# Gathers that read their row numbers from the table of slots, each after a wait on an event of VectorE

## The chip, the cores and the metric

The kernel runs on one core of a Trainium2 chip. The metric is the device time of one execution in microseconds (us), taken as the median of several runs. The core has five engines that run side by side: TensorE (PE in the profile, with PEld for its weight loads), VectorE (DVE), ScalarE (ACT), GpSimd (POOL) and SyncE (SP), the last of which only starts transfers here. They wait for each other by counters (semaphores): `engine.wait_ge(counter, value)`, and `.then_inc(counter, n)` on the instruction that raises it.

## The reference, cut to what matters

```
# x (50000, 128), src (25000,) node of each edge, edge_attr (25000, 128)
h   = relu(layernorm(x))                      # no weights
agg = segment_sum(edge_attr, src, 50000)      # (50000, 128)
g   = silu(concat([h, agg]) @ W1 + b1)        # W1 (256, 256)
g   = g @ W2 + b2                             # W2 (256, 128)
g   = layernorm(g) * ln_gamma + ln_beta
out = x + (g + h)
```

## The kernel before, in words

The nodes are worked through in 49 blocks (`NB`) of 1024 (`BLOCK`), a block as 8 tiles (`TILES`) of 128 rows, in two halves of 4 tiles (`HALF`, `c` = 0 and 1).

**The first stage**, up to about 123 us, sorts the edges: every tile of nodes gets 128 slots, and the table `slot_edge` [128, 392] holds the number of the edge that sits in each slot (one column for each tile), `slot_node` its node. VectorE writes the tables in two pieces (`slot_tables`): the columns of blocks 0 to 2, and all others, during block 0. Each piece raises `slots_ready` by one.

**The main stage** runs over the blocks. For one tile GpSimd fetches 128 rows of `edge_attr` by one indirect DMA (`gather`, L430) into `G`; VectorE makes a matrix of ones and zeros from the node numbers (`one_hots`, `HOT`, L861), and TensorE multiplies the two (`sum_edges`, L602), which gives the sums by node. Beside it ScalarE normalises x (`normalise`, L493) and TensorE turns the result (`turn_h`, L595). Both land in `za` in PSUM. ScalarE copies `za` rounded to `hi` (`split_high`, L500 and L502), VectorE writes the remainder to `lo` (`split_low`, L870). TensorE forms the first layer (`layer1`, L613, L614, L618) and the second (`layer2`, L626 once and L630 for each half), ScalarE the silu (L508) and the sums of squares (L515). VectorE scales (`scale`, L886), adds (`result`, L896), and has the sums with beta and with h (`x_plus_beta`, L853; `residual`, L878). A chain of small dependent operations for the reciprocal roots (`powers`, L729 to L752, one `small` count for each of 13 links) runs on VectorE too, with statistics of the next block (L697), one half of `HOT`, `x_plus_beta` and one `residual` put in between.

VectorE's order in `step(b)` is: `split_low(b, 1)`, `one_hots(b+1, 1)`, `scale(b-2)` for both halves, `result(b-2)` for both halves, `residual(b-1, 1)`, `split_low(b+1, 0)`, `powers(b+2)`. GpSimd does nothing but the gathers in the main stage. It works on block b+2 in its step b, and `G` has three buffers (`RING`), so `gather` waits on `agg_done` until the block three before has been summed. TensorE works on the halves in order; `turn_h` and `sum_edges` of a half stand ahead of `layer1` of the half before. The order on each engine is that of the program.

Around each gather GpSimd first copies one column of the table to a small tile (`name_row`, L418, `gather_rows`), one tile ahead of its use, and the gather waits for `row_named`, which the copy raises. Beside the case shown here there is one for more than 128 edges in a tile (`flag != 0`), which this input doesn't take; it gathers from `spill` by the same function.

Of the kernel before, what the change touches and what calls it, by code (L numbers as in the profile page):

```python
# [10 lines left out]
U32 = mybir.dt.uint32  # L11
# [4 lines left out]
P = 128  # L16
TILES = 8
HALF = TILES // 2
BLOCK = P * TILES
RING = 3  # L20
X_RING = 6
# [12 lines left out]
NEWTON = 3  # L34
# [55 lines left out]
def at_least(engine, semaphore, value):  # L90

    if value > 0:
        engine.wait_ge(semaphore, value)


def gnn_layer(nc, x, src, edge_attr, W1, b1, W2, b2, gamma, beta, out):
# [4 lines left out]
    NB = -(-nodes // BLOCK)  # L101
# [3 lines left out]
    FULL = edges // EC  # L105
    REST = edges - FULL * EC
    FIRST_BLOCKS = 3
    assert all((place + LAG_DVE_RANK) % BATCH == BATCH - 1 for place in DVE_RANKS)
    assert EC % UNROLL == 0 and UNROLL % STREAMS == 0 and NT <= 512

# [3 lines left out]
    with ExitStack() as ctx:  # L114
        def sb(name, shape, dt):
            return ctx.enter_context(nc.sbuf_tensor(name, shape, dt))
# [4 lines left out]
        def sem(name):  # L121
            return ctx.enter_context(nc.semaphore(name))
# [47 lines left out]
        slot_edge = sb("slot_edge", [P, NT], U32)  # L170
# [23 lines left out]
        R = [sb(f"R{j}", [P, TILES, D], F32) for j in range(RING)]  # L194
        G = [sb(f"G{j}", [P, TILES, D], F32) for j in range(RING)]
        HOT = [sb(f"HOT{j}", [P, TILES, P], F32) for j in range(RING)]
        gather_rows = [sb(f"gather_rows{j}", [P, TILES], U32) for j in range(X_RING)]

        hi = [sb(f"hi{c}", [P, 2, HALF * P], F32R) for c in range(2)]
        lo = [sb(f"lo{c}", [P, 2, HALF * P], F32R) for c in range(2)]  # L200
# [35 lines left out]
        spill_known, slots_ready = sem("spill_known"), sem("slots_ready")  # L236
        pool_step = sem("pool_step")
        spill_zeroed, spill_added = sem("spill_zeroed"), sem("spill_added")
        row_named = sem("row_named")
        x_loaded = [sem(f"x_loaded{j}") for j in range(X_RING)]  # L240
        stored = [sem(f"stored{j}") for j in range(RING)]
        gathered = [[sem(f"gathered{j}{c}") for c in range(2)] for j in range(RING)]
        bn_done, small, powers_done = sem("bn_done"), sem("small"), sem("powers_done")
        h0_done, turn_done, hot_done, agg_done = sem("h0_done"), sem("turn_done"), sem("hot_done"), sem("agg_done")
        hi_done, lo_done = sem("hi_done"), sem("lo_done")
        pre_done, silu_done, y_done = sem("pre_done"), sem("silu_done"), sem("y_done")
        squares_done = sem("squares_done")
        xb_done, r_done, t_done, out_done = sem("xb_done"), sem("r_done"), sem("t_done"), sem("out_done")
        pool_passed = sem("pool_passed")

        def run_blocks(step):

            for n in range(NB):
                step(Block(n))
# [68 lines left out]
        def _(pool):  # L323
# [85 lines left out]
                    pool.dma_reset(range(spill_added.num, spill_added.num + 1))  # L409
                    pool.sem_clear(spill_added)  # L410

            def name_row(b, t):

                if t == 0:
                    at_least(pool, agg_done, b.half(0, 1, 2 - 2 * X_RING))
                    if b.is_number(FIRST_BLOCKS):
                        pool.wait_ge(slots_ready, 2)
                nc.gpsimd.tensor_copy(gather_rows[b.xj][:, t:t + 1],  # L418
                                      slot_edge[:, bass.ds(b.number(TILES, t), 1)]).then_inc(row_named, 1)

            def gather(b, c, source, limit):

                at_least(pool, agg_done, b.half(0, 1, 2 - 2 * RING))
                for t in range(c * HALF, (c + 1) * HALF):
                    if t + 1 < TILES:
                        name_row(b, t + 1)
                    elif b.plus(1).exists(NB):
                        name_row(b.plus(1), 0)
                    at_least(pool, row_named, b.number(TILES, t + 1))
                    nc.gpsimd.indirect_dma_start(  # L430
                        G[b.j][:, t, :], None, source,
                        bass.IndirectOffsetOnAxis(ap=gather_rows[b.xj][:, t:t + 1], axis=0),
                        bounds_check=limit, oob_is_err=False).then_inc(gathered[b.j][c], 16)

            def gather_all(source, last):

                limit = pool.to_reg(last)
                for n in range(2):
                    for c in range(2):
                        gather(Block(n), c, source, limit)  # L440

                def step(b):
                    if b.plus(2).exists(NB):
                        for c in range(2):
                            gather(b.plus(2), c, source, limit)

                run_blocks(step)

            pool.wait_ge(late_const, 1)
            pool.wait_ge(slots_ready, 1)  # L450
            name_row(Block(0), 0)
            with pool.If(flag == 0):
                gather_all(edge_attr, edges - 1)
            with pool.If(flag != 0):
# [201 lines left out]
        def _(dve):  # L656
# [35 lines left out]
            def statistics(b, t):  # L692
# [4 lines left out]
                done = nc.vector.bn_stats(stats[b.ring(2)][:, t, :], X[b.xj][:, t, :])  # L697
                if t == TILES - 1:
                    done.then_inc(bn_done, 1)

            SMALLS = 4 + 3 * NEWTON

            def powers(b):

# [4 lines left out]
                def link_small(instruction):  # L709
# [8 lines left out]
                    if b.plus(-2).exists(NB) and not b.is_number(0) and not b.is_number(1):  # L718
                        if place in (TILES + 1, TILES + 2):
                            x_plus_beta(b.plus(-2), place - TILES - 1)  # L720
                        if place == TILES + 3:
                            residual(b.plus(-2), 0)
                    dve.wait_ge(small, b.number(SMALLS, count[0]))

# [120 lines left out]
            dve.wait_ge(words_placed, 2)  # L845
            slot_tables(0, FIRST_BLOCKS * TILES)

# [9 lines left out]
            def one_hots(b, c):  # L857
                if b.is_number(FIRST_BLOCKS) and c == 0:
                    dve.wait_ge(slots_ready, 2)
# [46 lines left out]
            def step(b):  # L906
# [3 lines left out]
                if b.is_number(0):  # L910
                    slot_tables(FIRST_BLOCKS * TILES, NT)
                elif not b.is_number(1):
# [43 lines left out]
```

## Time and profile before

| | us |
|---|---|
| median of 3 runs (800.46 to 802.87) | 801.94 |
| the profiled execution, its own time | 803.43 |
| its span, first to last instruction | 801.9 |
| PE busy (share of the span) | 733.6 (91%) |
| DVE busy | 732.1 (91%) |
| ACT busy | 587.0 (73%) |
| POOL busy | 601.1 (75%) |
| mean granted TensorE clock | 0.974 |

Busy is the time in which an engine has at least one instruction under way; neighbours on one engine overlap by some hundredths of a us. A matmul's end is modelled, so a busy PE isn't PE at its peak. The span is cut into stretches below, since the first 123 us (the sorting) are another program than the rest.

### The profile page before, as it was taken

The numbers are of one execution on the slowest core, as the hardware profiler recorded it, in microseconds if no ns is written. First come the engines' busy times: TensorE is split into PE (matmuls) and PEld (weight loads), VectorE is DVE, ScalarE is ACT, GpSimd is POOL, SyncE is SP. The second block draws the span as 40 slices with busy tenths as digits, with TensorE's granted clock in tenths as the row PEclk, the third lists the DMA queues.
The fourth block names the chain that finished last, engine by engine and source line by source line (L and its number), as shares of the span: only waits on it lengthen the run. The fifth ranks groups of instructions, "written<-read, shape, count | busy, mean of one in ns | idle before, by whom it ended". The sixth has DMA issues, their size and how long they took to land.

```text
span 801.9 us, 15882 instructions
## 1 busy us (share of the span) xinstructions
PE 733.6 (91%) x4567; PEld 592.4 (74%) x4616; DVE 732.1 (91%) x2494; ACT 587.0 (73%) x1927; POOL 601.1 (75%) x831
## 2 busy tenths in 40 slices
PE   4999993989999999999999999999999999989990
PEld 1455542878888888888888888888888888878880
DVE  6999995879999999999999999999999999989994
ACT  4999982767777777777777777777777777757860
POOL 4600006889998999889989998999989998989920
PEclk9999995999999999999999999999999999999996
DMA  5000000122323333332323232323233332321211
GB/s 191 2 1 2 1 0 17 48 74 75 124 90 110 98 103 99 102 120 80 126 74 126 74 125 74 127 78 121 91 107 100 102 107 93 126 66 51 71 61 48
DMA packets 28159, 65.86 MB, mean 82 GB/s; under 512 B 8379, under 2 KB 9934, under 8 KB 28070
## 3 DMA queue, kind: packets, MB, share of 16 engines
q1 hardware_dynamic: 15526, 51.90, 18.6%
q0 software_dynamic: 12544, 12.93, 6.5%
q8 instruction: 37, 0.61, 0.3%
q14 instruction: 52, 0.43, 0.2%
HBM read 51.98 MB, written 25.60 MB: 97 GB/s over the span
## 4 chain that ended last, share of the span: by engine, by line
POOL 66%; ACT 10%; issue 8%; PE 8%; DVE 5%; DMA 1%; SPq 0%; POOLq 0%; DVEq 0%
POOL G L430 50%; POOL gather_rows L418 16%; ACT junk_rank L472 10%; PE y L630 2%; PE za L602 1%; PE pre L613 1%; PE pre L614 1%; DVE hot_tile L768 1%; PE pre L618 1%; DVE hot_slot L790 1%; DVE T L886 1%; DMA srci<-in_src_dram 1%; DMA G<-in_edge_attr_dram,gather_rows 1%; PE za L595 0%; DVE is_slot L781 0%
## 5 line engine op out<-in xcount | busy, mean ns | idle before, releaser
L430 POOL DMA_INDIRECT G<-in_edge_attr_dram,gather_rows x392 | 440.6, 1124 | 63.4 <-POOL gather_rows L418 48.2
L418 POOL COPY gather_rows<-slot_edge 128x1 uint32<-128x1 uint32 x392 | 138.5, 354 | 92.0 <-DVE slot_edge L842 89.6
L630 PE MATMUL y<-w2c,S 128*128 128x128 f32 x1568 | 190.9, 275 | 3.3
L630 PEld LDWEIGHTS y<-w2c,S 128*128 128x128 f32 x1568 | 191.5, 192 | 2.5
L493 ACT ACTIVATE H<-X,shift,rstd 128x128 f32<-128x128 f32 x392 | 162.4, 508 | 7.7 <-DVE shift L752 7.6
L613 PE MATMUL pre<-hi,w1h 128*128 128x512 f32 x392 | 164.8, 420 | 0.4 <-issue 0.4
L870 DVE TENSOR_TENSOR lo<-za,hi 128x1024 fp32r<-128x1024 f32 x98 | 119.8, 1222 | 46.5 <-ACT hi L502 42.3
L614 PE MATMUL pre<-hi,w1l 128*128 128x512 f32 x392 | 156.1, 398 | 0.0
L500 ACT CAST hi<-za 128x512 fp32r<-128x512 f32 x98 | 57.4, 586 | 123.5 <-PE za L595 113.6
L602 PE MATMUL za<-HOT,G 128*128 128x128 f32 x784 | 114.4, 290 | 18.4 <-issue 10.1
L508 ACT ACTIVATE S<-pre,b1c 128x512 f32<-128x512 f32 x196 | 125.3, 697 | 5.0 <-remote 2.1
L602 PEld LDWEIGHTS za<-HOT,G 128*128 128x128 f32 x784 | 97.1, 195 | 37.4 <-DMA G<-in_edge_attr_dram,gather_rows 31.5
L618 PE MATMUL pre<-lo,w1h 128*128 128x512 f32 x392 | 124.0, 397 | 0.0
L697 DVE BATCH_NORM_STATS2 stat<-X 128x6 f32<-128x128 f32 x392 | 109.0, 284 | 0.0
L515 ACT ACTIVATE junk_sq<-y 128x128 bf16<-128x128 f32 x392 | 103.7, 286 | 3.5 <-PE y L630 3.5
L886 DVE SCALAR_TENSOR_TENSOR T<-y,rstd,gammas 128x128 f32<-128x128 f32 x392 | 105.6, 341 | 0.0
L502 ACT CAST hi<-za 128x512 fp32r<-128x512 f32 x98 | 57.6, 588 | 42.4 <-PE za L602 25.0
L618 PEld LDWEIGHTS pre<-lo,w1h 128*128 128x128 f32 x392 | 74.4, 190 | 18.1
L613 PEld LDWEIGHTS pre<-hi,w1h 128*128 128x128 f32 x392 | 75.0, 191 | 14.3 <-issue 0.8
L515 ACT ACTIVATION_READ_ACCUMULATOR junk_sq<-y 128x1 f32 x392 | 85.0, 217 | 0.0
L614 PEld LDWEIGHTS pre<-hi,w1l 128*128 128x128 f32 x392 | 75.0, 191 | 13.4
L595 PE MATMUL za<-ident,H 128*128 128x128 f32 x392 | 59.8, 276 | 13.4 <-ACT H L493 9.0
(123 smaller groups left out, 1047.3 us busy)
## 6 DMA issues: line engine op xcount, KB each, us to landing
X<-in_x_dram SPq DMA_DIRECT2D x48, 512.0 KB
out_dram<-R SPq DMA_DIRECT2D x48, 512.0 KB
G<-in_edge_attr_dram,gather_rows POOLq DMA_INDIRECT x392
X<-in_x_dram SPq DMA_DIRECT2D x1, 424.0 KB
out_dram<-R SPq DMA_DIRECT2D x2, 212.0 KB
w1f<-in_L_gnn_W_dram SPq DMA_DIRECT2D x1, 256.0 KB, 3.3
w2f<-in_L_gnn_W_dram SPq DMA_DIRECT2D x1, 128.0 KB, 2.6
srci<-in_src_dram SPq DMA_DIRECT2D x1, 97.2 KB
```

Source lines behind the costliest of these rows:

```text
L418: nc.gpsimd.tensor_copy(gather_rows[b.xj][:, t:t + 1], slot_edge[:, bass.ds(b.number(TILES, t), 1)]).then_inc(row_named, 1)
L430: nc.gpsimd.indirect_dma_start(G[b.j][:, t, :], None, source, bass.IndirectOffsetOnAxis(ap=gather_rows[b.xj][:, t:t + 1], axis=0), bounds_ ...
L493: done = nc.scalar.activation(H0[b.j][:, t, :], X[b.xj][:, t, :], ACT.Relu, bias=shift[b.j][:, t:t + 1], scale=rstd[b.j][:, t:t + 1])
L508: nc.scalar.activation(S[c][:, m, :], pre[m][:], ACT.Silu, bias=b1c[:, m:m + 1]).then_inc(silu_done, 1)
L515: done = nc.scalar.activation(junk_sq[:, p, c * HALF + t, :], y[2 * p + c][:, t * D:(t + 1) * D], ACT.Square, scale=float(D) ** -0.5, accu ...
L602: done = nc.tensor.matmul(za[:, 1, t * P:(t + 1) * P], G[b.j][:, c * HALF + t, :], HOT[b.j][:, c * HALF + t, :], start=True, stop=True)
L613: nc.tensor.matmul(pre[m][:], w1h[:, k, cols], hi[c][:, k, :], start=(k == 0), stop=False)
L614: nc.tensor.matmul(pre[m][:], w1l[:, k, cols], hi[c][:, k, :], start=False, stop=False)
L618: done = nc.tensor.matmul(pre[m][:], w1h[:, k, cols], lo[c][:, k, :], start=False, stop=(k == 1))
L630: done = nc.tensor.matmul(place[:, t * D:(t + 1) * D], S[c][:, m, t * P:(t + 1) * P], w2c[:, m, :], start=False, stop=(t == HALF - 1 and m ...
L870: nc.vector.tensor_tensor(out=lo[c][:], in0=za[:], in1=hi[c][:].bitcast(F32), op=ALU.subtract).then_inc(lo_done, 1)
L886: done = nc.vector.scalar_tensor_tensor(out=T[c][:, t, :], in0=y[2 * b.ring(2) + c][:, t * D:(t + 1) * D], scalar=rstd[b.j][:, n:n + 1], i ...
```

## The change

The tile `gather_rows`, the counter `row_named` and the function `name_row` are gone: 392 copies on GpSimd. The indirect DMA takes its 128 row numbers from the column of `slot_edge` itself. The gathers of blocks 0 and 1 wait for nothing new. From block 2 on, each of the 8 gathers of block b+2 has a wait of its own (`pace`), on an event of VectorE (in before's line numbers):

| gather | waits until this is done |
|---|---|
| half 0, 1st | `split_low(b, 1)` (L870) |
| half 0, 2nd | `scale(b-2, 0)` (L886) |
| half 0, 3rd | `result(b-2, 0)` (L896) |
| half 0, 4th | `residual(b-1, 1)` (L878) |
| half 1, 1st | `split_low(b+1, 0)` (L870) |
| half 1, 2nd | 3rd link of `powers(b+2)` (the one ahead of L741) |
| half 1, 3rd | 8th link of `powers(b+2)` |
| half 1, 4th | `x_plus_beta(b, 0)` (L853) |

The wait for the second piece of the tables moves to the first gather of block 3. `SMALLS` moves up in the file. Nothing changes on the other engines, in what they do or in its order.

```
-            def name_row(b, t):
-
-                if t == 0:
-                    at_least(pool, agg_done, b.half(0, 1, 2 - 2 * X_RING))
-                    if b.is_number(FIRST_BLOCKS):
-                        pool.wait_ge(slots_ready, 2)
-                nc.gpsimd.tensor_copy(gather_rows[b.xj][:, t:t + 1],
-                                      slot_edge[:, bass.ds(b.number(TILES, t), 1)]).then_inc(row_named, 1)
-
-            def gather(b, c, source, limit):
-
+            def pace(b, c, k):
+
+                if k == 0:
+                    at_least(pool, lo_done, b.half(1, 1, c + 1))
+                elif c == 0 and k == 1:
+                    at_least(pool, t_done, b.plus(-2).half(0, 1, 1))
+                elif c == 0 and k == 2:
+                    at_least(pool, out_done, b.plus(-2).half(0, 1, 1))
+                elif c == 0:
+                    at_least(pool, r_done, b.plus(-1).half(1, 1, 1))
+                elif k == 3:
+                    at_least(pool, xb_done, b.half(0, 1, 1))
+                else:
+                    at_least(pool, small, b.plus(2).number(SMALLS, 5 * k - 2))
+
+            def gather(b, c, source, limit, pacer=None):
+
+                if b.is_number(FIRST_BLOCKS) and c == 0:
+                    pool.wait_ge(slots_ready, 2)
                 at_least(pool, agg_done, b.half(0, 1, 2 - 2 * RING))
                 for t in range(c * HALF, (c + 1) * HALF):
-                    if t + 1 < TILES:
-                        name_row(b, t + 1)
-                    elif b.plus(1).exists(NB):
-                        name_row(b.plus(1), 0)
-                    at_least(pool, row_named, b.number(TILES, t + 1))
+                    if pacer is not None:
+                        pace(pacer, c, t - c * HALF)
                     nc.gpsimd.indirect_dma_start(
                         G[b.j][:, t, :], None, source,
-                        bass.IndirectOffsetOnAxis(ap=gather_rows[b.xj][:, t:t + 1], axis=0),
+                        bass.IndirectOffsetOnAxis(ap=slot_edge[:, bass.ds(b.number(TILES, t), 1)], axis=0),
                         bounds_check=limit, oob_is_err=False).then_inc(gathered[b.j][c], 16)
...
-                            gather(b.plus(2), c, source, limit)
+                            gather(b.plus(2), c, source, limit, pacer=b)
...
             pool.wait_ge(slots_ready, 1)
-            name_row(Block(0), 0)
```

What stands in a row on GpSimd in the middle of the main stage, before: copies and gathers taking turns.

```order
133 L418 COPY gather_rows<-slot_edge 128x1
134 L430 DMA G<-in_edge_attr_dram,gather_rows 128x128 [waits row_named]
135 L418 COPY gather_rows<-slot_edge 128x1 [waits agg_done]
136 L430 DMA G<-in_edge_attr_dram,gather_rows 128x128 [waits row_named]
137 L418 COPY gather_rows<-slot_edge 128x1
```

The same place in the changed program, one block's 8 gathers (`x2` stands for two alike).

```order
74 L434 DMA G<-in_edge_attr_dram,slot_edge 128x128 [waits lo_done,agg_done]
75 L434 DMA G<-in_edge_attr_dram,slot_edge 128x128 [waits t_done]
76 L434 DMA G<-in_edge_attr_dram,slot_edge 128x128 [waits out_done]
77 L434 DMA G<-in_edge_attr_dram,slot_edge 128x128 [waits r_done]
78 L434 DMA G<-in_edge_attr_dram,slot_edge 128x128 [waits lo_done,agg_done]
79 L434 DMA G<-in_edge_attr_dram,slot_edge 128x128 [waits small] x2
80 L434 DMA G<-in_edge_attr_dram,slot_edge 128x128 [waits xb_done]
```

The copies between the gathers are gone, and the waits now name VectorE's counters. At the head of the main stage the first 16 gathers, of blocks 0 and 1, follow one another.

```order
61 L455 COMPARE_AND_BRANCH [waits slots_ready,late_const]
62 L434 DMA G<-in_edge_attr_dram,slot_edge 128x128 x16
63 L434 DMA G<-in_edge_attr_dram,slot_edge 128x128 [waits lo_done]
64 L434 DMA G<-in_edge_attr_dram,slot_edge 128x128 x3
65 L434 DMA G<-in_edge_attr_dram,slot_edge 128x128 [waits lo_done]
```

VectorE's order around `split_low(b+1, 0)` (L870) and the beginning of `powers` is the same in both programs; it stands here by before's lines, since the prediction asks what lies beside the fifth and sixth gather of a block.

```order
1041 L878 TENSOR_TENSOR R<-H,R 128x512 [waits h0_done,xb_done]
1042 L870 TENSOR_TENSOR lo<-za,hi 128x1024 [waits pre_done,hi_done]
1043 L729 TENSOR_TENSOR msum<-stat 128x8 [waits bn_done,powers_done]
1044 L730 SCALAR_TENSOR_TENSOR m<-stat 128x8
1045 L732 TENSOR_TENSOR mdif<-stat 128x8
1046 L861 TENSOR_TENSOR HOT<-iota_node,slot_node 128x512 [waits agg_done]
1047 L734 SCALAR_TENSOR_TENSOR mdd<-mdif 128x8 [waits small]
1048 L697 BN_STATS stat<-X 128x6 [waits powers_done,x_loaded1]
1049 L737 TENSOR_SCALAR var<-meansq 128x8 [waits squares_done,small]
1050 L738 SCALAR_TENSOR_TENSOR var<-m,mdd 128x8
1051 L697 BN_STATS stat<-X 128x6
1052 L741 TENSOR_SCALAR guess<-var 128x16 [waits small]
```

Nothing moved here; the fifth gather is now released where L870 ends, and the sixth where L738 ends.

## Rows read from the trace of the kernel before

**Rows 1.** Page, chain that ended last, by line: share of the span.

```profile
POOL G L430 50%; POOL gather_rows L418 16%; ACT junk_rank L472 10%; PE y L630 2%; PE za L602 1%; PE pre L613 1%; PE pre L614 1%; DVE hot_tile L768 1%; PE pre L618 1%; DVE hot_slot L790 1%; DVE T L886 1%; DMA srci<-in_src_dram 1%; DMA G<-in_edge_attr_dram,gather_rows 1%; PE za L595 0%; DVE is_slot L781 0%
```

**Rows 2.** Waits in 300 to 700 us: waiter, releaser, us in total, times, longest.

```profile
DVE lo L870 <- ACT hi L502: 21.3, 31, 0.8
PEld za L602 <- DMA G<-in_edge_attr_dram,gather_rows: 18.7, 41, 0.7
```

**Rows 3.** Groups by line, 300 to 700 us: count, busy us, mean ns, idle before.

```profile
L430 POOL DMA_INDIRECT G<-in_edge_attr_dram,gather_rows x245 | 272.0, 1110 | 38.7 <-POOL gather_rows L418 31.5 <-issue 7.3
L418 POOL COPY gather_rows<-slot_edge 128x1 uint32<-128x1 uint32 x244 | 88.6, 363 | 1.4
```

**Rows 4.** Timeline, PEld: start us, duration us; one L626 stands in each half.

```profile
178.42 0.10 PEld L626 LDWEIGHTS y<-b2rows,ones 128*128 128x128 bf16 x1 [0.28 <-issue]
...
203.00 0.10 PEld L626 LDWEIGHTS y<-b2rows,ones 128*128 128x128 bf16 x1 [0.28 <-issue]
...
713.91 0.10 PEld L626 LDWEIGHTS y<-b2rows,ones 128*128 128x128 bf16 x1 [0.27 <-issue]
...
724.92 0.10 PEld L626 LDWEIGHTS y<-b2rows,ones 128*128 128x128 bf16 x1 [0.28 <-DVE T L886]
```

**Rows 5.** Timeline, GpSimd beside VectorE, from 401 us.

```profile
401.33 1.03 POOL L430 DMA_INDIRECT G<-in_edge_attr_dram,gather_rows  x1 [0.15 <-issue]
...
402.37 0.44 POOL L418 COPY gather_rows<-slot_edge 128x1 uint32<-128x1 uint32 x1
...
402.97 1.39 POOL L430 DMA_INDIRECT G<-in_edge_attr_dram,gather_rows  x1 [0.16 <-POOL gather_rows L418]
```

**Rows 6.** Timeline, VectorE, GpSimd and one of TensorE, 189 to 202 us.

```profile
189.04 1.22 DVE L870 TENSOR_TENSOR lo<-za,hi 128x1024 fp32r<-128x1024 f32 x1
...
190.38 1.66 POOL L430 DMA_INDIRECT G<-in_edge_attr_dram,gather_rows  x1 [0.16 <-POOL gather_rows L418]
...
195.81 1.22 DVE L870 TENSOR_TENSOR lo<-za,hi 128x1024 fp32r<-128x1024 f32 x1
...
198.87 0.60 PE L595 MATMUL za<-ident,H 128*128 128x128 f32 x4
...
201.42 1.22 DVE L870 TENSOR_TENSOR lo<-za,hi 128x1024 fp32r<-128x1024 f32 x1
```

**Rows 7.** Groups by line, VectorE: first 184.56 to 209.43 us, then 400 to 426 us.

```profile
L741 DVE TENSOR_SCALAR guess<-var 128x16 int32<-128x16 int32 x2 | 0.5, 256 | 0.0
L737 DVE TENSOR_SCALAR var<-meansq 128x8 f32<-128x8 f32 x2 | 0.5, 233 | 0.0
...
L741 DVE TENSOR_SCALAR guess<-var 128x16 int32<-128x16 int32 x2 | 0.3, 157 | 0.0
L737 DVE TENSOR_SCALAR var<-meansq 128x8 f32<-128x8 f32 x2 | 0.3, 154 | 0.0
```

**Rows 8.** Timeline, VectorE and GpSimd, at 726 and at 756 us.

```profile
725.88 1.28 DVE L896 TENSOR_TENSOR R<-T,R 128x512 f32<-128x512 f32 x2
725.93 2.73 POOL L430 DMA_INDIRECT G<-in_edge_attr_dram,gather_rows  x1 [0.16 <-issue]
...
755.58 1.66 POOL L430 DMA_INDIRECT G<-in_edge_attr_dram,gather_rows  x1 [0.15 <-POOL gather_rows L418]
...
756.79 0.42 DVE L741 TENSOR_SCALAR guess<-var 128x16 int32<-128x16 int32 x1
```

**Rows 9.** Timeline, PEld: sums that waited long for the gathered rows.

```profile
132.71 1.78 PEld L602 LDWEIGHTS za<-HOT,G 128*128 128x128 f32 x8 [2.40 <-DMA G<-in_edge_attr_dram,gather_rows]
...
157.81 0.97 PEld L602 LDWEIGHTS za<-HOT,G 128*128 128x128 f32 x8 [0.92 <-DMA G<-in_edge_attr_dram,gather_rows]
...
719.53 1.52 PEld L602 LDWEIGHTS za<-HOT,G 128*128 128x128 f32 x8 [3.25 <-DMA G<-in_edge_attr_dram,gather_rows]
```

**Rows 10.** Timeline, ScalarE at 168 us: the wait ahead of L500.

```profile
167.64 0.59 ACT L500 CAST hi<-za 128x512 fp32r<-128x512 f32 x1 [4.32 <-remote]
```

**Rows 11.** Instructions on the tile HOT: L861, ns min/median/max.

```profile
L861 DVE TENSOR_TENSOR HOT<-iota_node,slot_node x98: 678/683/740, 123.5 to 761.8; 128x512 f32<-128x512 f32 x98
```

More of the change, by code:

```diff
@@ L107, in gnn_layer @@
     FIRST_BLOCKS = 3
+    SMALLS = 4 + 3 * NEWTON
     assert all((place + LAG_DVE_RANK) % BATCH == BATCH - 1 for place in DVE_RANKS)
@@ L196, in gnn_layer @@
         HOT = [sb(f"HOT{j}", [P, TILES, P], F32) for j in range(RING)]
-        gather_rows = [sb(f"gather_rows{j}", [P, TILES], U32) for j in range(X_RING)]
         hi = [sb(f"hi{c}", [P, 2, HALF * P], F32R) for c in range(2)]
@@ L238, in gnn_layer @@
         spill_zeroed, spill_added = sem("spill_zeroed"), sem("spill_added")
-        row_named = sem("row_named")
         x_loaded = [sem(f"x_loaded{j}") for j in range(X_RING)]
@@ L699, in statistics @@
                     done.then_inc(bn_done, 1)
-            SMALLS = 4 + 3 * NEWTON
             def powers(b):
```

## The prediction, made before the changed kernel ran

> **What bounds the kernel now.** I read the chain that ended last first. Two thirds of the span lie on GpSimd: 50% on the gathers, 16% on the copies ahead of them [rows 1]. The waits of the middle 400 us come next. TensorE's weight loads wait for gathered rows 41 times, 18.7 us in all; VectorE waits 31 times, once a block, for ScalarE's `hi` [rows 2]. GpSimd waits for its own copies and for nothing else of weight [rows 3]. So it works without a pause and sets the pace. The groups by line give its bill: 245 gathers (30.6 blocks of 8) with 272.0 us busy, 244 copies with 88.6 us, and 38.7 us idle ahead of the gathers, most of it the step from a copy to its gather [rows 3]. Together 400 us in 400, or 13.06 us a block: 8.9 in gathers, 2.9 in copies, 1.3 in between.
>
> How fast would the rest go? TensorE's load L626 stands once in each half. From 203.00 to 713.91 there are 78 halves, 39 blocks, 510.9 us, or 13.10 us a block. From 178.42 to 203.00, while the gathers were still ahead, four halves take 24.58 us, or **12.29 us a block** [rows 4]. That is TensorE without a wait for rows.
>
> VectorE is hardly faster. From one L870 to the next but one (189.04, 195.81, 201.42) it takes 6.77 and 5.61 us, 12.38 us a block, without a pause [rows 6]. This holds some delay by GpSimd: L741 and L737 take 256 and 233 ns there, but 157 and 154 ns at 400 us [rows 7], 0.18 us together. Without it VectorE needs 12.20 us.
>
> **Removing the copies.** 8 copies of 363 ns and 8 steps of 0.16 us [rows 3] leave GpSimd's chain, 4.2 us a block. What is left is 8.9 us of gathers. The step from one gather to the next isn't in this trace. From below it is nothing; from above I take the 0.16 us of copy to gather, since nothing more is waited for. The block then costs GpSimd 8.9 to 10.2 us, under 12.29 by at least 2.1. One gather that is held up as the longest of all (2.73 us [rows 8], 1.7 over the usual 1.03 [rows 5]) still fits. GpSimd stops being the bound, and next are TensorE (12.29) and VectorE (12.20 and what the gathers cost it).
>
> Reading from the large table instead of a small tile: no gather here does that. The 128 numbers are the same four bytes in each partition, so I take nothing; a gain isn't to be had where the small tile's gathers start with the same read. Its upper price is a rival below.
>
> **The waits.** Behind a waiting gather stand only gathers, and they run for block b+2 in step b. The last one of a step is released by `x_plus_beta(b, 0)`, about a block ahead of its `sum_edges`; a gather of 1.4 us [rows 5] fits in that. So the waits cost TensorE nothing. Even the stall at 719.53, where the rows came 3.25 us late [rows 9], would be covered.
>
> What they do set is what each gather meets on VectorE. Rows 5 show one direction: a gather usually takes 1.03 us, but 1.39 us where `x_plus_beta` (two inputs in SBUF) runs as it starts; the copy ahead of it was held in the same way, 0.44 us for 0.20. That costs only GpSimd, which now has room. The other direction matters: L741 takes 0.42 us beside the 1.66 us gather at 755.58, and ends at 757.21, with it (757.24) [rows 8]. The late part of a gather holds back this operation of VectorE with one input and one output in SBUF. [...]
>
> The fifth gather of a block is the one to look at. It is released at the end of L870, and the order shows L737 and L741 behind it. The trace has this very place: the gather of 190.38 started 0.12 us after L870's end (189.04 + 1.22 = 190.26), was held to 1.66 us by L861 [rows 6], and L741 took 0.26 us [rows 7]. That is the stretch with 12.38 us a block. A gather released there by the event would start at about the same point, so **I take 12.38 us a block for VectorE**. The ends: 12.20 where the gather falls elsewhere, since the fourth gather may push it past L741, and 12.70 where L737 and L741 together wait 0.5 us (both would have to meet the last part of one gather; L741 alone lost 0.26 us in the worst row). The sixth gather starts where L741 starts, and its late part comes after it.
>
> **The sum**, against the profiled span of 801.9 us:
> - 39 blocks from 13.10 to 12.29 us: 510.9 − 479.3 = 31.6 saved.
> - VectorE is 0.09 us a block slower than TensorE, 3.5 us over 39 blocks. `lo` was ready 1.8 us ahead of the next `turn_h` in the unhindered stretch (L870 ends at 197.03, L595 starts at 198.87 [rows 6]; an estimate for the new kernel), so the first 1.8 us are hidden: 1.7 lost.
> - The late rows at 719.53: the half that ends with L626 at 724.92 took 11.01 us instead of 6.15 [rows 4]: 4.9 saved, the lower clock after the wait included.
> - Start: the wait of 0.92 at 157.81 goes [rows 9]; block 2's gathers no longer queue behind copies. The first sum waited 2.40 us at 132.71 [rows 9]; four gathers without three or four steps of 0.35 us (copy and step) land 1.0 to 1.4 us earlier, and the first one may start some tenths earlier. I take 1.4, together 2.3 saved.
> - The pause ahead of ScalarE's L500 at 167.64, 4.32 us [rows 10], isn't released by a gather. I leave it.
>
> 801.9 − 31.6 + 1.7 − 4.9 − 2.3 = 764.8 us of span. The profiled execution's own time was 803.4, which gives 766.3; it lay 1.5 us above the median of the runs, so the predicted median is 765 us.
>
> **Rivals.**
> 1. *TensorE alone is the bound*: VectorE stays at or under 12.29 because the fifth gather starts late enough. For it: where a gather begins close ahead of two additions that follow each other (L896), it is held through them, 2.73 us [rows 8], and the third gather is released among these. Against it: the fourth might then be held by L861 instead. No 1.7: 763 us; 759 if the pause of rows 10 moves away as well.
> 2. *The late part of a gather costs VectorE 0.5 us every block*, 12.70 us: 39 × 0.41 − 1.8 = 14.2 lost instead of 1.7, 777 us. For it: the waits tie gather and operation together, so what was chance happens in every block. Against it: 0.26 us is the most that L741 lost.
> 3. *Reading from the large table is slower*, which ends slower than before. GpSimd is the bound again once a gather with its step costs over 13.1 / 8 = 1.64 us on average, 0.37 us more than 10.2 / 8. If the read cost 0.5 us more, as much again as half a gather, a block is 10.2 + 4.0 = 14.2 us and the 39 blocks cost 43 us more: about 838 us, allowing the 2.3 at the start. No row speaks for it.
> 4. *A gather holds VectorE for its whole length.* VectorE starts its next operation beside every release; if all 8 gathers kept one waiting 0.9 us, the block would be 12.20 + 7.2 = 19.4 us, some 1040 us. Against it: the longest of 98 L861 took 740 ns against a least of 678 [rows 11], 0.06 us more. [...]
> 5. *It doesn't do what it should*: a wait reaches so late an event that rows are late as before, about 800 us. The order shows each wait on an event of step b for block b+2, which leaves a block.
>
> **How the numbers follow.** Forecast 765 (12.3 to 12.5 us a block): 50%. Rival 1: 20%. Rival 2, or between it and the forecast: 22%. Rival 3: 2%, rival 4: 1%, rival 5: 2%. Gains of another kind between 778 and 799, for instance new pauses like that of rows 10: 3%. The range goes from 758, rival 1 with the pause gone, to 777, rival 2 whole. Within 0.3% of before (2.4 us, about what can be told from no change) only rival 5 ends: 2%. Slower: 3%. Faster: 95%.
>
> **What would show it.** After: no L418; gathers busy about 9 to 10 us a block with idle time ahead of them that VectorE ends; no wait of L602 for rows in the main stage; L626 every 6.15 to 6.2 us; VectorE's idle time ahead of L870 small or gone, with 12.3 to 12.4 us from one L870 to the next but one. L741 at 0.16 to 0.2 us means rival 1, at 0.4 and more rival 2. A gather of 1.5 us and more away from VectorE's additions means rival 3. The forecast fails if the period is set by something that no row shows, such as a transfer held by the stores now that gathers run a block ahead, or if the clock is granted differently with TensorE busier.

## The result, and the profile after

| | before | after |
|---|---|---|
| median of the runs, us | 802.40 (4 runs, 800.46 to 803.43) | 761.94 (4 runs, 761.75 to 762.03) |
| ratio | | 0.9498 [0.9479, 0.9517] |
| span of the profiled execution | 801.9 | 760.4 |
| PE busy, share of the span | 733.6, 91% | 711.6, 94% |
| DVE busy | 732.1, 91% | 727.7, 96% |
| POOL busy | 601.1, 75% | 481.0, 63% |
| mean granted TensorE clock | 0.974 | 0.978 |

The change takes 5.0% off. The forecast was 765 us, in a range from 758 to 777. The page of after has the chain that ended last, as shares of the span, by engine and by line:

```profile
PE 79%; ACT 11%; DVE 5%; issue 2%; DMA 1%; POOL 0%; SPq 0%; POOLq 0%; DVEq 0%
PE y L633 23%; PE pre L616 12%; PE pre L621 12%; PE pre L617 12%; PE za L605 12%; ACT junk_rank L475 10%; PE za L598 6%; PE y L629 1%; DVE hot_tile L769 1%; DVE hot_slot L791 1%; DVE T L887 1%; DMA srci<-in_src_dram 1%; POOL G L434 0%; DVE is_slot L782 0%; DMA G<-in_edge_attr_dram,slot_edge 0%
```

The chain lay on GpSimd for two thirds [rows 1]; now GpSimd has nothing of it and TensorE 79%. The waits from 300 to 700 us say the same (waiter, releaser, us in total, times, longest):

```profile
POOL G L434 <- issue: 69.0, 206, 1.0
ACT hi L503 <- PE za L598: 62.5, 65, 1.0
...
POOL G L434 <- DVE R L897: 8.0, 17, 0.5
POOL G L434 <- DVE lo L871: 6.9, 12, 1.3
POOL G L434 <- DVE guess L751: 5.8, 19, 0.3
POOL G L434 <- DVE T L887: 3.7, 2, 1.8
POOL G L434 <- DVE guess_sq L748: 1.8, 6, 0.3
```

TensorE no longer waits for rows, and VectorE no longer for `hi` [rows 2]; the only engine that the list shows waiting for TensorE is ScalarE, once for each of its two casts to `hi` in a half. GpSimd's waits on the five events of VectorE add up to 26.2 us in 400. Most of its idle time is "issue": nothing that the profile shows. The windows of the same stretch (PE, PEld, DVE, ACT and POOL busy, granted clock, DMA share, GB/s) show two engines without room, TensorE and VectorE, at the full clock:

```profile
300.00:700.00 400.00, 397.82 (x2633) 350.36 (x2664) 398.86 (x1391) 317.47 (x1038) 305.20 (x262) 1.00 0.33 105
```

L629, the old L626, gives the length of a half [rows 4]. Timeline of after, PEld (start, duration):

```profile
166.06 0.10 PEld L629 LDWEIGHTS y<-b2rows,ones 128*128 128x128 bf16 x1 [0.28 <-issue]
172.22 0.10 PEld L629 LDWEIGHTS y<-b2rows,ones 128*128 128x128 bf16 x1 [0.28 <-issue]
...
196.86 0.10 PEld L629 LDWEIGHTS y<-b2rows,ones 128*128 128x128 bf16 x1 [0.28 <-issue]
...
677.34 0.10 PEld L629 LDWEIGHTS y<-b2rows,ones 128*128 128x128 bf16 x1 [0.28 <-issue]
683.50 0.10 PEld L629 LDWEIGHTS y<-b2rows,ones 128*128 128x128 bf16 x1 [0.28 <-issue]
```

From 166.06 to 732.78, every half takes 6.16 us. The 78 halves from 196.86 to 677.34 take 480.5 us, where before took 510.9: 12.32 us a block for 13.10.

Last, GpSimd in one block (after, timeline, engine POOL), the first seven of its eight gathers, without the second:

```profile
400.62 0.99 POOL L434 DMA_INDIRECT G<-in_edge_attr_dram,slot_edge  x1 [0.70 <-issue]
...
403.38 1.80 POOL L434 DMA_INDIRECT G<-in_edge_attr_dram,slot_edge  x1 [0.47 <-DVE R L897]
405.49 1.00 POOL L434 DMA_INDIRECT G<-in_edge_attr_dram,slot_edge  x1 [0.30 <-issue]
406.79 1.00 POOL L434 DMA_INDIRECT G<-in_edge_attr_dram,slot_edge  x1 [0.30 <-issue]
408.10 1.00 POOL L434 DMA_INDIRECT G<-in_edge_attr_dram,slot_edge  x1 [0.31 <-DVE guess L751]
409.40 1.52 POOL L434 DMA_INDIRECT G<-in_edge_attr_dram,slot_edge  x1 [0.30 <-issue]
```

and what VectorE does beside the third to the fifth and the seventh of them (after, timeline, engine DVE):

```profile
402.43 1.28 DVE L897 TENSOR_TENSOR R<-T,R 128x512 f32<-128x512 f32 x2
403.63 0.69 DVE L879 TENSOR_TENSOR R<-H,R 128x512 f32<-128x512 f32 x1
404.31 1.23 DVE L871 TENSOR_TENSOR lo<-za,hi 128x1024 fp32r<-128x1024 f32 x1
...
406.92 0.15 DVE L742 TENSOR_SCALAR guess<-var 128x16 int32<-128x16 int32 x1
...
408.66 0.68 DVE L854 TENSOR_TENSOR R<-X,betas 128x512 f32<-128x512 f32 x1
...
410.04 0.68 DVE L879 TENSOR_TENSOR R<-H,R 128x512 f32<-128x512 f32 x1
```

Three things are to be seen. A gather that nothing holds takes 0.99 to 1.00 us, and the step to the next one takes 0.30. The third gather, released by the first half of L897, runs into its second half and L879, and takes 1.80. That moves the fourth to 405.49 and the fifth to 406.79, 0.13 us ahead of L742 (L741 before), which is over, in 0.15 us, before the gather's late part comes. The other blocks are alike in this. Some gather is held in each, for 1.67 to 2.28 us, until 2.74 to 2.77 us after the first L897 begins; and from 172 to 703 us one always begins 0.04 to 0.23 us ahead of L742, which takes 0.14 to 0.17 us. L742 was longer only three times: at 149.37 and 160.51 (0.31 each), where it begins 0.85 and 0.78 us behind the start of a gather and ends with it, within 0.03 us, and at 714.79 (0.23), between two gathers.

### The profile page after: what moved, and what is told of

Its sections match the earlier page's. It is cut to its first block, busy times and chain, and to the rows that moved or that the text cites. A ratio compares the mean times of both kernels' runs of the same rounds, so it can differ in the third digit from the quotient of the medians.

```text
span 760.4 us, 15582 instructions
## 1 busy us (share of the span) xinstructions
PE 711.6 (94%) x4567; PEld 588.6 (77%) x4616; DVE 727.7 (96%) x2494; ACT 586.0 (77%) x1927; POOL 481.0 (63%) x439
## 4 chain that ended last, share of the span: by engine, by line
PE 79%; ACT 11%; DVE 5%; issue 2%; DMA 1%; POOL 0%; SPq 0%; POOLq 0%; DVEq 0%
PE y L633 23%; PE pre L616 12%; PE pre L621 12%; PE pre L617 12%; PE za L605 12%; ACT junk_rank L475 10%; PE za L598 6%; PE y L629 1%; DVE hot_tile L769 1%; DVE hot_slot L791 1%; DVE T L887 1%; DMA srci<-in_src_dram 1%; POOL G L434 0%; DVE is_slot L782 0%; DMA G<-in_edge_attr_dram,slot_edge 0%
## 5 line engine op out<-in xcount | busy, mean ns | idle before, releaser
L434 POOL DMA_INDIRECT G<-in_edge_attr_dram,slot_edge x392 | 459.0, 1171 | 227.0 <-issue 198.3
L871 DVE TENSOR_TENSOR lo<-za,hi 128x1024 fp32r<-128x1024 f32 x98 | 119.7, 1222 | 9.8 <-ACT hi L505 9.7
L605 PE MATMUL za<-HOT,G 128*128 128x128 f32 x784 | 105.6, 278 | 1.6 <-DMA G<-in_edge_attr_dram,slot_edge 1.6
L879 DVE TENSOR_TENSOR R<-H,R 128x512 f32<-128x512 f32 x98 | 66.8, 681 | 0.0
```

Of the source, the lines that this page charges most:

```text
L434: nc.gpsimd.indirect_dma_start(G[b.j][:, t, :], None, source, bass.IndirectOffsetOnAxis(ap=slot_edge[:, bass.ds(b.number(TILES, t), 1)], a ...
L605: done = nc.tensor.matmul(za[:, 1, t * P:(t + 1) * P], G[b.j][:, c * HALF + t, :], HOT[b.j][:, c * HALF + t, :], start=True, stop=True)
L871: nc.vector.tensor_tensor(out=lo[c][:], in0=za[:], in1=hi[c][:].bitcast(F32), op=ALU.subtract).then_inc(lo_done, 1)
```

## The experiments

The question after the result: what sets the 12.32 us a block, which part of the change brought it, and where did the 4.5 us come from that the sum didn't have? The theory: TensorE sets the time, GpSimd's eight copies were what kept it from doing so, and the waits and the place that the numbers are read from are worth nothing. The rivals: VectorE's rhythm or the waits set the period, or reading straight from the table is a gain of its own. Ratios are to the kernel before on the same chip.

### Before once more

The kernel before, unchanged, for the pause of rows 10.

> The kernel before, unchanged, profiled a second time. It asks whether the pause of 4.3 us ahead of ScalarE's L500 at 167.64 us and the late rows at 719.53 us belong to the program. If they do, both stand at the same places within 0.5 us, and the time is 800 to 803 us. If the pause is chance, it is elsewhere or missing, and a trace without it spans 797 to 798 us.

803.7 us, span 802.2. Timeline, PEld:

```profile
167.36 0.10 PEld L626 LDWEIGHTS y<-b2rows,ones 128*128 128x128 bf16 x1 [0.27 <-issue]
174.10 0.10 PEld L626 LDWEIGHTS y<-b2rows,ones 128*128 128x128 bf16 x1 [0.27 <-issue]
...
200.34 0.10 PEld L626 LDWEIGHTS y<-b2rows,ones 128*128 128x128 bf16 x1 [0.27 <-issue]
...
714.37 0.10 PEld L626 LDWEIGHTS y<-b2rows,ones 128*128 128x128 bf16 x1 [0.27 <-issue]
...
720.03 0.97 PEld L602 LDWEIGHTS za<-HOT,G 128*128 128x128 f32 x8 [3.29 <-DMA G<-in_edge_attr_dram,gather_rows]
```

There is no pause here: the half from 167.36 takes 6.74 us, where the profiled execution of before had 10.69 (167.73 to 178.42). TensorE reaches 200.34 2.66 us earlier than it reached 203.00, and still it stands at 714.37 where it stood at 713.91 [rows 4]. So the pause comes in one execution and not in another, and, as far as these two show, it cost the kernel before nothing: GpSimd went on gathering beside it (it idled at most 0.16 us ahead of a gather), and TensorE had to wait for rows later on in any case. The expectation, that a trace without the pause would span 797 to 798 us, missed. The late rows ahead of the ninth half from the end, in contrast, are there both times (3.29 us at 720.03; 3.25 in rows 9).

### The waits taken out

```
-                            gather(b.plus(2), c, source, limit, pacer=b)
+                            gather(b.plus(2), c, source, limit)
```

> The changed kernel without the 8 waits on VectorE: gathers follow one another, held only by the three buffers of G. Theory: removing the copies does it all, since TensorE (12.32 us a block in the trace after) is the bound and VectorE has 0.1 us a block to spare; then the time is within 1.5 us of the changed kernel, 762 to 763.5 us. Rival: the waits keep the late part of the gathers off VectorE's L738 and L742; without them VectorE needs 12.4 to 12.6 us a block, L742 takes 0.25 us and more, and the time is 766 to 774 us.

761.56 us, ratio 0.9483 [0.9465, 0.9502]: the same as with the waits. Halves take 6.16 us again. GpSimd and VectorE of this kernel, timeline:

```profile
439.52 2.27 POOL L434 DMA_INDIRECT G<-in_edge_attr_dram,slot_edge  x1 [0.30 <-issue]
...
451.83 2.26 POOL L434 DMA_INDIRECT G<-in_edge_attr_dram,slot_edge  x1 [0.30 <-issue]
```

```profile
439.03 1.29 DVE L897 TENSOR_TENSOR R<-T,R 128x512 f32<-128x512 f32 x2
440.23 0.69 DVE L879 TENSOR_TENSOR R<-H,R 128x512 f32<-128x512 f32 x1
```

In every block from 205 to 716 us a gather begins among the three additions (L897 twice, L879), and is held until 0.87 us after the last of them (439.52 + 2.27 = 441.79 against 440.92). These long gathers stand 12.31 us apart, a block of TensorE's. Nothing in the program ties GpSimd to VectorE here, but being held does. Wherever in the additions the gather begins, it ends 2.75 to 2.77 us after the start of the first of them. In 36 of these 42 blocks it begins 0.5 us behind that start and takes 2.26 or 2.27 us; in the other six it begins 1.1 us behind and takes 1.66 to 1.68. The one at 378.65 is such a gather, with an L897 at 377.56:

```profile
368.13 1.00 POOL L434 DMA_INDIRECT G<-in_edge_attr_dram,slot_edge  x1 [0.30 <-issue]
...
378.65 1.66 POOL L434 DMA_INDIRECT G<-in_edge_attr_dram,slot_edge  x1 [0.30 <-issue]
```

The eight gathers from 368.13 up to it met none of the three additions and took 10.52 us, not 12.3. Such an eight, of 10.51 to 10.53 us, occurs seven times in the kernel. So GpSimd only looks full (320 us busy and 80 of issue in 400); it has nearly 2 us a block to spare.

### The waits alone, with the copies kept

The kernel before, with `pace` as in the change, ahead of the wait for `row_named`:

```
+                    if pacer is not None:
+                        pace(pacer, c, t - c * HALF)
                     at_least(pool, row_named, b.number(TILES, t + 1))
```

> The kernel before with its copies, and the 8 waits added. Theory: GpSimd stays the bound at 13.06 us a block; the waits are mostly satisfied when it comes to them, and the time is 798 to 806 us. Rival: the waits place copies and gathers away from VectorE's additions, GpSimd is held up less (0.1 us for each of 8 pairs), and the time falls to 770 to 790 us. A third way: every wait costs GpSimd its own issue on a full engine, 0.1 to 0.3 us each, and the time rises to 820 us and more.

806.74 us in 8 runs, ratio 1.0044 [1.0029, 1.0059]: 3 us slower than before. The groups by line, 300 to 700 us (count, busy us, mean ns, idle before):

```profile
L448 POOL DMA_INDIRECT G<-in_edge_attr_dram,gather_rows x242 | 268.0, 1107 | 42.3 <-POOL gather_rows L419 37.8 <-issue 4.5
L419 POOL COPY gather_rows<-slot_edge 128x1 uint32<-128x1 uint32 x241 | 89.9, 373 | 1.5
```

Against rows 3 there are 242 gathers for 245 in the same 400 us, and 3.6 us more of idle time. That idle time isn't spread over the waits: it lies in three gaps, 159 us apart, at 309.35, 468.57 and 627.81 us, 1.5 us each, 4.5 us together; the first (timeline, POOL):

```profile
309.35 1.04 POOL L448 DMA_INDIRECT G<-in_edge_attr_dram,gather_rows  x1 [1.51 <-issue]
```

Behind the first gather of the main stage neither trace of before has an idle time over 0.30 us ahead of a gather. The remaining steps from copy to gather are 0.16 us, as before (37.8 us for 239, against 31.5 for 198). A wait that is met thus shows no price of its own. The profile doesn't show what the engine did in the gaps, and no run tells whether they account for the whole 3 us. The waits don't help, in any case: the rival with 770 to 790 us is out.

### One copy for eight

The kernel before with its copies merged: one of 8 columns for each block.

```
-                nc.gpsimd.tensor_copy(gather_rows[b.xj][:, t:t + 1],
-                                      slot_edge[:, bass.ds(b.number(TILES, t), 1)]).then_inc(row_named, 1)
+                nc.gpsimd.tensor_copy(gather_rows[b.xj][:],
+                                      slot_edge[:, bass.ds(b.number(TILES), TILES)]).then_inc(row_named, 1)
...
-                    at_least(pool, row_named, b.number(TILES, t + 1))
+                    if t == 0:
+                        at_least(pool, row_named, b.number(1, 1))
```

> The kernel before with one copy of 8 columns a block in place of 8 copies of one column, no waits on VectorE. It parts the number of copies from where the gather reads. Theory: what counts is the number of instructions between gathers; GpSimd needs 8 x 1.3 us, one copy of 0.4 us and 1 to 1.5 us of holding, 12.3 us a block at most, and the time is 762 to 768 us. Rival: reading from the table is itself faster than from the small tile (1.00 against 1.03 us); then gathers stay at 1.03 us here, 0.24 us a block more, which shows in GpSimd's busy time but in the time by under 2 us.

760.75 us, ratio 0.9467 [0.9449, 0.9486]: the whole gain, though the gathers still read from `gather_rows`. Groups by line, 300 to 700 us:

```profile
L428 POOL DMA_INDIRECT G<-in_edge_attr_dram,gather_rows x261 | 320.2, 1227 | 74.9 <-issue 69.5 <-POOL gather_rows L417 5.4
L417 POOL COPY gather_rows<-slot_edge 128x8 uint32<-128x8 uint32 x33 | 6.6, 199 | 0.1
```

A copy of 8 columns takes 199 ns, no more than the 0.20 of an unheld copy of one. A gather from `gather_rows` that stands behind another gather takes 1.00 us here, as those from the table do; the one right behind the copy takes 1.03 (at 389.63, for instance). So the 1.03 of before belongs to the copy ahead, not to the place that is read. What the change removes is instructions; where the gather reads its numbers has no price that can be seen, either way. The time is 1.3 us under the expected range; at least part of this is the shorter half of 6.147 us, taken up at the end of this section.

### No gathers

```
-                    if b.plus(2).exists(NB):
+                    if b.is_number(0):
...
-                pe.wait_ge(gathered[b.j][c], b.lap(16 * HALF, 16 * HALF))
+                pe.wait_ge(gathered[b.j][c], 16 * HALF)
```

> The changed kernel with the gathers of blocks 3 to 48 left out (their sums use the rows that lie in the buffers). GpSimd is idle from block 3 on. Theory: TensorE alone sets 12.3 us a block, so the time stays within 1 us of the changed kernel, 761 to 762 us. Rival: gathers still cost something through VectorE or the transfers; then it falls to 755 to 759 us.

761.99 us, ratio 0.9489 [0.9467, 0.951]. Windows:

```profile
300.00:700.00 400.00, 400.00 (x2665) 350.35 (x2664) 398.35 (x1392) 318.01 (x1040) 0.00 (x0) 1.00 0.24 84
```

Without one gather on GpSimd (x0) the time is the same, with 6.16 us a half. GpSimd, its gathers' transfers and what they do to VectorE cost the changed kernel nothing that can be told. VectorE's busy time doesn't fall either (398.86 to 398.35): it follows TensorE, and its busy share doesn't tell whether it could go faster.

### The fourth gather released later

To have the late part of the fourth gather fall on L742, it is released later, by the next `split_low` as the fifth is:

```
                 elif c == 0:
-                    at_least(pool, r_done, b.plus(-1).half(1, 1, 1))
+                    at_least(pool, lo_done, b.half(1, 1, 2))
```

> The changed kernel with one wait changed: the fourth gather of a block waits for split_low(b+1, 0) instead of residual(b-1, 1). It then starts beside L862 and its late part falls on L742. Theory of the prediction (the late part of a gather holds L742): L742 takes 0.3 to 0.45 us instead of 0.15, VectorE needs 12.5 to 12.6 us a block, TensorE waits for lo after some ten blocks, and the time is 768 to 776 us. Rival: the rhythm gives way elsewhere and VectorE keeps 12.3 us; the time is 761 to 763 us.

761.8 us, ratio 0.9487 [0.9466, 0.9508]: no change. Timeline, POOL and DVE:

```profile
405.92 1.46 POOL L434 DMA_INDIRECT G<-in_edge_attr_dram,slot_edge  x1 [0.54 <-DVE lo L871]
```

```profile
404.44 1.21 DVE L871 TENSOR_TENSOR lo<-za,hi 128x1024 fp32r<-128x1024 f32 x1
...
407.04 0.31 DVE L742 TENSOR_SCALAR guess<-var 128x16 int32<-128x16 int32 x1
...
411.20 1.22 DVE L871 TENSOR_TENSOR lo<-za,hi 128x1024 fp32r<-128x1024 f32 x1
...
416.81 1.22 DVE L871 TENSOR_TENSOR lo<-za,hi 128x1024 fp32r<-128x1024 f32 x1
```

The collision is there: L742 at 407.04 takes 0.31 us and ends at 407.35, with the gather (405.92 + 1.46 = 407.38), and VectorE's block is 6.76 + 5.61 = 12.37 us, the forecast's value. But it is only 0.05 us over TensorE's 12.32, so the 2.2 us that `lo` is ahead of its use wear off by some hundredths a block. Over four such blocks they went from 2.17 to 1.93; then, one block on, the gathers fell out of this place by themselves. In all, L742 was held in 15 of the 45 blocks from 160 to 703 us (0.31 or 0.32 us), at most six in a row. A run of a whole main stage at 12.37 would lose 39 × 0.05 = 2 us, about what is hidden. The expectation, with 12.5 to 12.6 us a block and 768 to 776 us, missed; the rival's 761 to 763 us came.

### A shorter TensorE

The matmul that adds b2 (L629) is left out, to see what is next.

```
-                nc.tensor.matmul(place[:], ones16[:], b2rows[:].rearrange("p t d -> p (t d)"), start=True, stop=False)
...
-                                                w2c[:, m, :], start=False, stop=(t == HALF - 1 and m == 1))
+                                                w2c[:, m, :], start=(m == 0), stop=(m == 1))
```

> The changed kernel without the matmul that adds b2 (L629), so b2 is left out of the result. TensorE needs 0.23 us a half less, 5.93 us, 11.86 us a block. It asks what is next behind TensorE. VectorE at 12.22 to 12.3 us a block should take over: 755 to 760 us. If GpSimd (9.3 us in gathers, 2.4 us between them, and its holding) is at its end too, gathered rows come late and the time is 760 us or more. Only if neither is near would the time fall by 49 x 0.46 = 22 us to 740 us.

757.01 us, ratio 0.943 [0.941, 0.9451]. Waits, 300 to 700 us, and two L870 25 blocks apart in VectorE's timeline:

```profile
ACT H L496 <- DVE shift L752: 44.3, 32, 1.5
...
PEld za L598 <- ACT H L496: 12.0, 32, 0.4
```

```profile
384.64 1.22 DVE L870 TENSOR_TENSOR lo<-za,hi 128x1024 fp32r<-128x1024 f32 x1
...
690.51 1.22 DVE L870 TENSOR_TENSOR lo<-za,hi 128x1024 fp32r<-128x1024 f32 x1
```

Now ScalarE waits for VectorE's `powers` and TensorE for ScalarE's H, once a block: VectorE sets the time. (690.51 − 384.64) / 25 = 12.23 us a block is VectorE's own least, with the gathers running beside it. The changed kernel's two bounds are thus 12.32 (TensorE) and 12.23. The 757.01 us lie in the expected 755 to 760.

### An unused tile in the place of `gather_rows`

The unhindered halves of before took 6.145 us [rows 4], those of the merged copies 6.147, and those of after, with and without waits or gathers, 6.160. The first two have `gather_rows` (six tiles of 32 bytes a partition) between `HOT` and `hi`. Three kernels, and the changed one once more beside two of them, tell whether that is what counts: the changed one with an unused tile of that size in the old place, the one without waits with the same line, and the changed one with it behind `S`, so that only what lies behind `hi`, `lo` and `S` is moved back.

```
         HOT = [sb(f"HOT{j}", [P, TILES, P], F32) for j in range(RING)]
+        unused = [sb(f"unused{j}", [P, TILES], U32) for j in range(X_RING)]
```

> The changed kernel with an unused tile of the size of gather_rows at its place, so that every tile behind it lies at the address it has in the kernel before. In the traces a half takes 6.160 us wherever gather_rows is gone (the changed kernel and the one without waits) and 6.145 us where it is there. Theory: the addresses of TensorE's or ScalarE's operands make the 0.015 us; then the halves take 6.145 us and the time is 1.5 us less, 760.3 to 760.8 us. Rival: reading the row numbers from the large table does it; then it stays at 761.6 to 762.1 us.

> The changed kernel without the waits on VectorE and with the unused tile at the place of gather_rows. If both earlier readings hold (the waits do nothing for the time, the addresses give 0.0135 us a half), halves take 6.147 us and the time is 760.2 to 761.0 us, as with the unused tile and the waits. If the waits protect something that showed only by chance, it is 762 us and more.

> The changed kernel with the unused tile behind S instead of ahead of hi: hi, lo and S keep the addresses of the changed kernel, T and all behind it those of the kernel before. If the addresses of hi and lo, which layer1 streams, make the slower half, it stays at 6.160 us (762 us). If it is those of T or behind, it falls to 6.147 us (760.8 us).

> The changed kernel itself, beside the two others on one chip, so that 1 us can be told: 761.7 to 762.1 us and halves of 6.160 us.

| kernel | median, us | ratio | span | a half, us |
|---|---|---|---|---|
| unused tile ahead of `hi` | 760.84 | 0.9479 [0.9458, 0.95] | 759.0 | 6.147 |
| the same, no waits | 760.12 | 0.9469 [0.9449, 0.9488] | 758.5 | 6.147 |
| unused tile behind `S` | 761.68 | 0.9486 [0.9467, 0.9505] | 760.0 | 6.160 |
| changed, once more | 762.02 | 0.949 [0.9469, 0.9511] | 760.7 | 6.160 |

The halves are 78 apart in the timeline of each, as (675.61 − 196.17) / 78 = 6.147 in the second. The groups on PE from 200 to 700 us, of the second and then of the changed kernel once more (count, busy us, mean ns):

```profile
L617 PE MATMUL pre<-hi,w1h 128*128 128x512 f32 x327 | 136.1, 416 | 0.0
...
L622 PE MATMUL pre<-lo,w1h 128*128 128x512 f32 x328 | 103.0, 395 | 0.0
```

```profile
L616 PE MATMUL pre<-hi,w1h 128*128 128x512 f32 x326 | 136.5, 419 | 0.0
...
L621 PE MATMUL pre<-lo,w1h 128*128 128x512 f32 x324 | 102.4, 397 | 0.0
```

The matmuls that stream `hi` and `lo` against `w1h` are 3 and 2 ns longer, and there are four of each in a half: 20 ns by these rounded and overlapping durations, where the half is 13 ns longer. Those that stream `hi` against `w1l` take 395 ns in both. The kernels without waits, with one copy, and with the tile behind `S` fall in with this: 419 and 397 ns where a half takes 6.160 us, 416 and 395 where it takes 6.147. The difference follows the place of `hi`, `lo` or `S`, 192 bytes a partition further on or not: all kernels on one side of it have 6.147 and all on the other 6.160. By medians alone it would be doubtful, since the intervals of the ratios overlap; the periods don't. Why the place matters stays open, as does which of the three tiles it is, though the groups speak for `hi` and `lo`. Set beside kernels with the same addresses, the merged copy (760.75 us) and the gathers from the table (760.84 and 760.12) can't be told apart.

## Why the prediction was right, and where it wasn't

The time came out 3 us under the forecast, the span 4.4 us (760.4 for 764.8). By its own steps, with the places in the two traces:

| stretch | before | after | saved | predicted |
|---|---|---|---|---|
| up to the load at 167.73 / 166.06 | | | 1.7 | 2.3 |
| the next half (10.69 / 6.16) | to 178.42 | to 172.22 | 4.5 | 0 |
| 4 halves to 203.00 / 196.86 | 24.6 | 24.6 | 0 | 0 |
| 39 blocks | 510.9 | 480.5 | 30.4 | 31.6 − 1.7 = 29.9 |
| the half of the late rows | 11.01 | 6.16 | 4.9 | 4.9 |
| sum, of the span | 801.9 | 760.4 | 41.5 | 37.1 |

The forecast's 4.9 for the late rows includes a lower clock behind them: from 719.5 to 725 us before had a granted clock of 0.69 (0.69 in its second trace too), after has 1.00 from 714 to 725.

- **What bound the kernel, and that the copies were the way to free it: right.** GpSimd left the chain; merging the copies alone brings the whole gain. The two parts of the change that were taken at nothing, the waits and the table, are worth nothing (no waits: 761.56; one copy: 760.75).
- **The pause of rows 10: this is the step that failed.** "I leave it" kept 4.5 us in the sum, for the reason that no gather releases it. Run again, before had no pause there and was no faster (803.7 us for 803.43). GpSimd was the path, and TensorE stood at the same place by 714 us with the pause and without it, so the pause, as far as two executions tell, was no part of the 801.9; and in after, where it would have counted, it isn't there. Its cause stays open.
- **12.38 us a block for VectorE: the mechanism was real, the place was not.** The forecast had the fifth gather at the end of L871. The third, held to 1.80 us, pushes it to 0.13 us ahead of L742, and L742 takes 0.15 us. By the prediction's own sign ("0.16 to 0.2 us means rival 1") rival 1 is what happened, by nearly the way it names, a gather released among additions. Where the collision was forced, it had the forecast's size (12.37), and the slack of `lo` covered it.
- **TensorE's 12.29: 12.32 here.** 39 × 0.03 = 1.2 us more, from the address of `hi`, `lo` or `S`, which no row of before could show. It happened to stand in for most of the 1.7 that VectorE didn't cost: luck, as far as the number goes. In spans, the forecast's 764.8 less the 4.5 of the pause and the 1.7 of VectorE, with this 1.2 and the 0.6 that the start fell short, is the 760.4 measured. The median is off by less, 3 us, for a reason that has nothing to do with the kernel: the forecast took 1.5 us off, since the profiled execution of before lay that much over the median known then, and the profiled execution of after lies at its median.
- **GpSimd's 8.9 to 10.2 us a block: too low.** The step between gathers is 0.30 us, not up to 0.16: 8 × 1.30 = 10.4 us where nothing holds them. The rest, up to 12.3 (305.2 us busy and 95.1 idle fill the 400), is being held by additions or waiting, and that gives way when needed (10.52 us in the quickest block without waits). The conclusion stood, but the margin of 2.1 us was about 1.8.
- **What a copy cost was read too simply.** Before, a copy and a gather that nothing holds made a turn of 407.75 − 406.37 = 1.38 us (before, timeline, engine POOL):

```profile
406.37 1.03 POOL L430 DMA_INDIRECT G<-in_edge_attr_dram,gather_rows  x1 [0.16 <-POOL gather_rows L418]
407.40 0.20 POOL L418 COPY gather_rows<-slot_edge 128x1 uint32<-128x1 uint32 x1
407.75 1.03 POOL L430 DMA_INDIRECT G<-in_edge_attr_dram,gather_rows  x1 [0.15 <-issue]
```

A gather alone makes 1.30. So an unheld copy adds only 0.08: it takes 0.35 us with the step behind it, in place of the 0.30 of issue, and the gather behind it takes 1.03 in place of 1.00. What made copies dear is that they are held too (363 ns on average [rows 3] for 0.20). GpSimd's turn of 13.06 us a block was 8 × 1.38 = 11.0 and 2.0 of holds; 8 × 1.30 = 10.4 and the same holds is 12.4, even a little over TensorE's 12.32. So, by this sum, taking the copies away wouldn't have freed GpSimd if the holds had stayed; that they give way is seen in the kernel without waits (10.52 us), and why they didn't give way in before is not shown.
- **Rivals 2 to 5 are out.** L742 keeps to 0.14 to 0.17 us in all but three blocks and costs nothing even at 0.31; the gathers from the table take 1.00 us, not more than 1.03; two additions that begin while a gather runs, L854 at 408.66 (gather of 408.10) and L879 at 410.04 (gather of 409.40), take 0.68 us each, the least of L861 too [rows 11], and no L854 or L879 of the whole trace takes over 0.69. (Rival 3's 838 us doesn't follow from its terms: 801.9 + 43 − 2.3 is 843; 838 also takes off the 4.9 of the late rows.) Between gathers and additions the holding goes in one direction in these runs: the additions hold a gather to 1.80 us (after, 403.38) and to 2.27 us (without the waits, 439.52) where an unheld one takes 1.00, and a gather that has begun doesn't hold an addition (0.68 us). What decides which of VectorE's operations a gather does hold, as it held L742 (0.31 us for 0.15), is not shown.

## What to carry to other kernels

On the engine that sets the pace, count instructions before looking at what they read: eight copies of one column became one of eight at no loss, and that brought all of the gain. A pause that lies off the path that sets the end belongs in no sum, neither as a cost that stays nor as one to be won; look whether the same point is reached later at the same time in another execution. Once a bound is taken away, price the next two together: here TensorE (12.32 us a block) and VectorE (12.23) are less than 1% apart, and with these two as they are little more than 5% was to be had.

## What the hardware showed that was not expected

- Between two indirect DMAs on GpSimd lie 0.30 us of issue, and an unheld copy of 0.20 us in between adds only 0.08 (a turn of 1.38 us with it, 1.30 without).
- A gather that starts among VectorE's three additions (L897 twice, L879) ends 2.74 to 2.77 us after the first of them begins, so it takes up to 2.28 us for 1.00. Without the waits too, GpSimd falls into VectorE's rhythm by it (the long gathers stand 12.31 us apart) and looks busy, 320 us in 400, with nearly 2 us a block to spare.
- A shift of `hi`, `lo` and `S` by 192 bytes a partition changes a half on TensorE from 6.147 to 6.160 us, 1.3 us over the kernel. The quickest kernels are those with the shorter half: 760.12 us (ratio 0.9469) for the changed one without waits and with an unused tile ahead of `hi`, 760.75 (0.9467) for the merged copies; these two can't be told apart.
